# Two cross-attentions on one core: the small algebra in four parts, and a reordered front

## The reference, cut to what matters

```
att = softmax(q k^T / 4) v        # 16 heads; q from x, k and v from ctx
y   = x + att[0]                  # one 256 x 256 block for all 32 batches
F   = layernorm(y) * w2 + b2      # queries
X   = layernorm(ctx) * w1 + b1    # keys and values
A   = softmax(F X^T / 16) X       # 32 batches
h   = gelu(A @ fc1^T + fc1_b)     # 4 features wide
c   = h @ fc2^T + fc2_b
n   = layernorm(c) * w3 + b3
s   = softmax(n n^T / 16) n
out = F + gamma2 * (c + gamma1 * s)
```

## Time and profile before

| | us |
| --- | --- |
| median of 3 runs | 240.56 |
| lowest and highest | 238.62, 248.52 |
| the profiled execution: time | 240.99 |
| its span, first to last instruction | 239.2 |
| PE, DVE, ACT, POOL busy | 213.3, 188.0, 151.0, 139.9 |
| mean granted TensorE clock, share of full | 0.957 |

### The profile page before, as it was taken

One profiled execution on the slowest core, in us unless ns is written; L12 is line 12 of the kernel. 1 busy time (PEld: TensorE's weight loads), 2 busy tenths in 40 slices (PEclk: granted clock), 3 DMA queues, 4 the chain that ended last, 5 costly groups with the idle time before them and its releaser, 6 DMA issues.

```text
span 239.2 us, 4947 instructions
## 1 busy us (share of the span) xinstructions
PE 213.3 (89%) x1736; PEld 153.9 (64%) x1736; DVE 188.0 (79%) x363; ACT 151.0 (63%) x292; POOL 139.9 (58%) x212
## 2 busy tenths in 40 slices
PE   6999989697999999999999989999997499899750
PEld 6766656574977969779698786877684254455320
DVE  6888876999999988968799998971354655988773
ACT  2067774406678858678586995876587346777520
POOL 6000068576999999979959993900028888222330
PEclk9999999979999999999999999999999956999995
DMA  6990000055550454415455000000000004264458
GB/s 191 380 348 7 1 1 3 3 182 169 167 179 29 162 171 176 152 51 160 171 171 174 6 3 1 3 0 1 3 0 3 1 13 165 106 243 182 176 205 325
DMA packets 14712, 26.81 MB, mean 112 GB/s; under 512 B 1760, under 2 KB 1760, under 8 KB 14688
## 3 DMA queue, kind: packets, MB, share of 16 engines
q1 hardware_dynamic: 14688, 26.50, 32.3%
HBM read 18.11 MB, written 8.39 MB: 111 GB/s over the span
## 4 chain that ended last, share of the span: by engine, by line
PE 58%; DVE 24%; POOL 7%; issue 5%; ACT 5%; DVEq 0%; ACTq 0%; POOLq 0%
PE psum L1040 15%; PE psum L977 7%; DVE bn L372 6%; DVE xN L392 5%; PE psum L1048 5%; PE psum L932 3%; DVE Fall L586 3%; PE psum L1078 2%; PE psum L1155 2%; PE psum L990 2%; PE psum L1060 2%; PE psum L1188 2%; PE psum L947 2%; PE psum L1005 2%; PE psum L1018 2%
## 5 line engine op out<-in xcount | busy, mean ns | idle before, releaser
L1040 PE MATMUL psum<-XT,Fall 128*128 128x256 f32 x256 | 62.5, 389 | 1.7 <-ACT Fall L822 1.7
L1040 PEld LDWEIGHTS psum<-XT,Fall 128*128 128x128 f32 x256 | 47.3, 195 | 7.5 <-ACT Fall L822 2.2
L665 POOL TENSOR_SCALAR cN<-cN,nmean,rstd 128x256 f32<-128x256 f32 x64 | 38.2, 608 | 2.4 <-POOL rstd L652 2.3
L645 POOL TENSOR_TENSOR xN<-xN,tgt 128x512 f32<-128x512 f32 x28 | 35.7, 1277 | 1.6 <-DVE xN L392 1.6
L392 DVE TENSOR_SCALAR xN<-xN,bn,rstd 128x256 f32<-128x256 f32 x64 | 34.0, 575 | 0.7 <-POOL rstd L652 0.7
L845 ACT ACTIVATE PT<-psum 128x512 f32<-128x512 f32 x32 | 19.2, 599 | 24.3 <-PE psum L1048 24.2
L652 POOL TENSOR_TENSOR rstd<-vps,minus_half 128x8 f32<-128x8 f32 (+1 forms) x16 | 25.0, 1564 | 15.7 <-DVE vps L383 15.6
L852 ACT ACTIVATE E<-psum,nmax 128x256 f32<-128x256 f32 x64 | 26.8, 474 | 11.0 <-DVE nmax L531 10.9
L531 DVE TENSOR_REDUCE nmax<-psum 128x2 f32<-128x512 f32 x32 | 21.9, 685 | 13.9 <-PE psum L1040 13.4
L571 DVE TENSOR_REDUCE nm<-psum 128x4 bf16<-128x1024 f32 x16 | 19.5, 1221 | 12.0 <-PE psum L1123 12.0
L819 ACT ACTIVATE XT<-psum,b1s,w1s 128x512 f32<-128x512 f32 x32 | 23.1, 792 | 3.7 <-PE psum L977 3.7
(11 more groups left out here) (174 smaller groups left out, 361.0 us busy)
## 6 DMA issues: line engine op xcount, KB each, us to landing
cN<-ctx SPq DMA_DIRECT2D x32, 256.0 KB, 2.9
xN<-x SPq DMA_DIRECT2D x32, 256.0 KB, 4.0
out<-Fall SPq DMA_DIRECT2D x32, 256.0 KB, 2.3
x0T<-x0t SPq DMA_DIRECT2D x1, 256.0 KB, 2.7
wqT<-wqt SPq DMA_DIRECT2D x1, 256.0 KB, 3.2
c0T<-c0t SPq DMA_DIRECT2D x1, 256.0 KB, 3.8
wkT<-wkt SPq DMA_DIRECT2D x1, 256.0 KB, 5.6
wvT<-wvt SPq DMA_DIRECT2D x1, 256.0 KB, 5.8
```

The lines of the kernel that those rows point to most:

```text
L645: pool.tensor_tensor(xN[:, b % SLOTS, :], xN[:, b % SLOTS, :], tgt2[:, :, :].rearrange("p t d -> p (t d)"), ALU.add).then_inc(y_ok, 1)
L665: pool.tensor_scalar(own, own, nmean[:, p % 4, NT * m + t:NT * m + t + 1], root_of(p, 0, m, t), ALU.add, ALU.mult)\
L1040: last = pe.matmul(bank[SBANK1[b % 3]][:, t * N:(t + 1) * N], Fall[:, b, c, t * P:(t + 1) * P], XT[:, p % 4, c, m * N:(m + 1) * N], start= ...
```

## The change

**The algebra.** It is done in four parts of 16 tiles. `hidden_input(0)`, `hidden(0)` take three parts (48 tiles) at once, in slots 27 and 29; part 3 has its own in the second attention (`hidden_input(1)` on DVE behind `maxima(1)`, `hidden(1)` on ACT behind `maxima_turned(2)`). The product with K is taken from h by POOL (`keyed`, 5 columns wide) and multiplied by the inverse root afterwards, in DVE's `left(k)`, which also adds K's last column. Parts 0 and 1 have their squares, variances and roots on DVE, parts 2 and 3 on POOL. `turn(p)` waits for left and right parts at p = 0, 4, 8 and 12; `turn(0)` moves from slot 30 to 31, `turn(1)` and `scores(0)` from 31 to behind the last batch.

**The front.** EARLY is 4: four pairs have the context treated in stage one, where each pair has its own variances and its own root. K is projected and masked in halves, value projections move, x0T and c0T are issued by ACT, and SP issues all context batches ahead of x. The output operand is computed by POOL and not by DVE. `project(0)` and `project_back(0)` come ahead of the slots, with the matmuls for Q and K between them, and slots 0 to 3 of DVE have an order of their own. POOL's addition 5 waits for four normalized batches.

```diff
-LATE = {20: (0,), 22: (1,), 23: (2,), 24: (3,), 25: (4,), 26: (5,), 27: (6,), 28: (7,), 29: (8,)}
+PART = TILES // 4
+SHARES = (slice(0, 3 * PART), slice(3 * PART, TILES))
+KEYED = (4, 8, 16, 24)
+EARLY = 4
...
-        output_operand(0)
-        dve.wait_ge(k_mm, 1)
-        for e, m in enumerate(("even", "odd")):
-            dve.tensor_scalar(kTm[:, e, :, :], tiles(bank[1]), c_(m), None, ALU.mult).then_inc(kT_ok, 1)
-        dve.wait_ge(qk_mm, 1)
-        output_operand(1)
+        def masked(o):
+            dve.wait_ge(k_mm, o + 1)
+            for e, m in enumerate(("even", "odd")):
+                dve.tensor_scalar(kTm[:, e, o, :], bank[(1, 5)[o]][:, 0:N], c_(m), None, ALU.mult).then_inc(kT_ok, 1)
+        masked(0)
...
+                if p == 0:
+                    masked(1)
+                statistics(p, 0)
+                if p % 2 == 1:
+                    first_variances(p // 2)
...
+        def left(k):
+            G = members(k)
+            dve.wait_ge(summed_ok, KEYED[k])
+            if k >= 2:
+                dve.wait_ge(rooted_ok, 7 * (k - 1))
+            link(dve.tensor_tensor(uK[:, G, :], uK[:, G, :], spread(r3[:, G], U), ALU.mult))
+            link(dve.tensor_tensor(uK[:, G, :], uK[:, G, :],
+                                   K[:, U * (U - 1):U * U].unsqueeze(1).to_broadcast([P, PART, U]), ALU.add))
             left_cuts(uK[:, G, :], cut[:, G, 0:U], sU[:, 0, G, :], U)
...
+        dve.wait_ge(qk_mm, 1)
+        link(dve.tensor_copy(Q[:, :], bank[7][:, 0:(H + 1) ** 2]))
+        link(dve.tensor_copy(K[:, :], bank[7][:, 64:64 + U * U]), "QK")
         normal(0)
...
-            if k + 3 < PAIRS:
+            if b >= 4 and k + 3 < PAIRS:
                 statistics(b + 6, 0)
                 statistics(b + 6, 1)
...
+            if b == 0:
+                statistics(5, 1)
+                variances(2)
+            elif b == 1:
+                statistics(6, 1)
+                normal(4)
+                normal(5)
+                statistics(7, 1)
+                variances(3)
+            elif b == 2:
+                statistics(8, 0)
+                statistics(8, 1)
+                normal(6)
+                normal(7)
+            elif b == 3:
+                statistics(9, 0)
+                statistics(9, 1)
+                variances(4)
+            elif k + 2 < PAIRS:
                 normal(b + 4)
-            for part in LATE.get(b, ()):
-                algebra(0, part)
+            if b == 27:
+                hidden_input(0)
+            if b == 29:
+                squares(0)
+                variance(0)
+            if b == 30:
+                scaled(0)
+            if b == 31:
+                left(0)
...
+        squares(1)
         maxima(0)
         saved(QUADS - 1)
+        variance(1)
+        scaled(1)
         for p in range(2 * QUADS + 5):
             if p + 1 < PAIRS:
                 maxima(p + 1)
...
+            if p == 0:
+                left(1)
+                hidden_input(1)
+            if p == 5:
+                left(2)
+            if p == 9:
+                left(3)
             if p >= 5:
                 finish(p - 5)
-            if p == 0:
-                algebra(1, 0)
-            if p == 4:
-                second_keyed(0)
-                second_left(0)
-            if p == 7:
-                second_left(1)
...
+            if b == 5:
+                pool.wait_ge(zy_ok, 8)
...
+        keyed(0)
+        keyed(1)
         right(0)
-        weights5()
-        scaled(0)
+        squares(2)
         right(1)
+        keyed(2)
+        scaled(2)
         output_cuts(0)
-        scaled(1)
+        right(2)
+        pool.wait_ge(gelu_ok, 2)
+        squares(3)
         output_cuts(1)
-        keyed(1)
-        right(2)
-        for q in range(2, QUADS):
+        scaled(3)
+        output_cuts(2)
+        right(3)
+        keyed(3)
+        for q in range(3, QUADS):
             output_cuts(q)
...
+            if b == 29:
+                hidden(0)
             if b >= 1:
                 weights_copied(b - 1)
             exponentials(b)
-            if b == 21:
-                hidden(0)
...
-            if p == 1:
+            if p == 2:
                 hidden(1)
...
-        keep_busy(11, 7)
+        project(0)
+        operand_products()
+        keep_busy(3, 0)
+        project_back(0)
+        keep_busy(4, 0)
         turned(0, 1)
```

More of the change, by code:

```diff
@@ L270, in _ @@
         sp.dma_start(par[:, :], params).then_inc(par_in, 16)
[L271 to L277, removed]
+        sp.dma_start(wqT[:, :, :], wqt).then_inc(q_in, 16)
+        sp.dma_start(wkT[:, :, :], wkt).then_inc(k_in, 16)
+        sp.dma_start(wvT[:, :, :], wvt).then_inc(v_in, 16)
+        for src, dst, arrived in ((c_d, cN, c_in), (x_d, xN, x_in)):
+            for b in range(SLOTS):
+                sp.dma_start(dst[:, b, :], src[b, :, :]).then_inc(arrived[b], 16)
+        for p in range(SLOTS // 2, PAIRS):
+            sp.wait_ge(t_mm, turns_to(p - SLOTS // 2, 1))
             for src, dst, arrived in ((c_d, cN, c_in), (x_d, xN, x_in)):
@@ new lines, in variance @@
+        def variance(k):
+            G = members(k)
+            w5, v, y = W5[:, G, :], var[:, G], r3[:, G]
+            link(dve.tensor_tensor(w5, w5, ha[:, G, :], ALU.mult))
+            link(dve.tensor_reduce(v, w5, AX.X, ALU.add))
+            link(dve.tensor_scalar(v, v, EPS, None, ALU.add))
+            link(dve.tensor_scalar(y.bitcast(I32), v.bitcast(I32), 1, None, ALU.logical_shift_right))
+            link(dve.tensor_scalar(y.bitcast(I32), y.bitcast(I32), -1.0, RSQRT_SEED, ALU.mult, ALU.add))
@@ new lines, in scaled @@
+        def scaled(k):
+            G = members(k)
+            for _ in range(NEWTON):
+                newton(var[:, G], r3[:, G], t3[:, G])
+            link(dve.tensor_tensor(u[:, G, 0:H + 1], ha[:, G, :], spread(r3[:, G], H + 1), ALU.mult), ("u", k))
+        def left(k):
+            G = members(k)
+            dve.wait_ge(summed_ok, KEYED[k])
[4 more added lines that the diff above has]
+                                   K[:, U * (U - 1):U * U].unsqueeze(1).to_broadcast([P, PART, U]), ALU.add))
+            left_cuts(uK[:, G, :], cut[:, G, 0:U], sU[:, 0, G, :], U)
+            ALG["left", k] = count[0]
@@ L523, in _ @@
         normal(3)
-        statistics(5, 1)
-        variances(2)
         def maximum(b):
@@ L782, in _ @@
     def _(act):
+        act.dma_start(x0T[:, :, :], x0t).then_inc(q_in, 16)
+        act.dma_start(c0T[:, :, :], c0t).then_inc(k_in, 16)
         act.wait_ge(q_mm, 1)
@@ L941, in _ @@
         last.then_inc(mean_mm, 1)
-        for arrived, n, w, src, b, done in ((q_in, 32, wqT, x0T, 0, q_mm), (k_in, 32, wkT, c0T, 1, k_mm)):
-            pe.wait_ge(arrived, n)
-            for o in range(2):
-                for c in range(DC):
-                    last = pe.matmul(bank[b][:, o * N:(o + 1) * N], w[:, c, o * P:(o + 1) * P], src[:, c, :],
-                                     start=c == 0, stop=c == DC - 1)
-            last.then_inc(done, 1)
+        pe.wait_ge(q_in, 32)
+        for o in range(2):
+            for c in range(DC):
+                last = pe.matmul(bank[0][:, o * N:(o + 1) * N], wqT[:, c, o * P:(o + 1) * P], x0T[:, c, :],
+                                 start=c == 0, stop=c == DC - 1)
+        last.then_inc(q_mm, 1)
+        pe.wait_ge(k_in, 32)
+        for o in range(2):
+            for c in range(DC):
+                last = pe.matmul(bank[(1, 5)[o]][:, 0:N], wkT[:, c, o * P:(o + 1) * P], c0T[:, c, :],
+                                 start=c == 0, stop=c == DC - 1)
+            last.then_inc(k_mm, 1)
         def operand_products():
@@ L1212, in _ @@
                 weights_turned(b - 1)
+            if b == B:
+                scores(0)
+                turn(1)
             if b == 29:
                 pe.wait_ge(evac_ok, 62)
-                pe.wait_ge(alg, ALG["stR"])
+                pe.wait_ge(operand_ok, ALG["stR"])
                 for c in range(DC):
```

275 lines of the change are left out of this document (113 added, 162 removed).

## The result

The changed kernel takes **259.61 us** (median of 4 runs, 259.08 to 261.53), the kernel before 239.75 beside it. The ratio is **1.083**, interval 1.078 to 1.087: 8% slower, and 10 us above the upper end of the range. Executions of one kernel fall into a faster and a slower state; every ratio here is taken over the faster ones, against the kernel before run beside it, so it can differ a little from the quotient of two medians. The profiled execution took 259.79 with a span of 258.0.

A forecast was written before the change was run, and what follows sets the result against it. PE bounds 60 to 116 us; later DVE and POOL chains set the pace. Stage one -1.15, to slot 6 -1.65, slots 20 to 28 -1.2, second attention +8.0: +4.0 on 240.99 gives 245.0 us, range 238 to 249.5.

The forecast's parts named there:

- the last of POOL's paragraph: Second attention: part 3's keys at 215.6, after maxima 10; DVE waits about 2 us; maxima 11 at 218.6, 8.0 late.
- rival E: Second attention: clock stays up, POOL's chain still binds, maxima 3 at 187.3; 241 to 243 us; chance 0.15.
- Rival C: Second attention: slow clock comes twice, PE standing again before left 3 or during hidden 1; 4 more, 249; chance 0.15.
- the sum: DVE's chain, slot 31 to maxima 2: left 0 and left 1 counted at 1.8 us each.
- its +8.0: Second attention: lateness of maxima 11, with DVE waiting about 2 us for POOL's keys of part 3; end follows at old pace.
- The prediction's own sign that its sum was too low: Second attention: if PE waits for left 1 or left 2 instead of left 3, the sum is too low.
- the 4.0 counted: Front's gain, taken off the forecast's dates: 1.15 stage one, 1.65 to slot 6, 1.2 slots 20 to 28.
- The wait of about 1 us ahead of slot 6: Slot 6: PE waits about 1 us for POOL's two normalizations, because the root stands behind two additions.
- The end of stage one: Stage one: first scores 2.05 early, part given back to added DVE steps, leaving 1.15; ends 2.05 and 0.
- The walk: The forecast's dates followed through the kernel, from the front to the end of the second attention, to a span of 243.3.
- POOL's five terms: POOL's work behind output cuts 0: cuts three times, right twice, squares, scaled, keyed: 5.5 + 4.8 + 2.4 + 5.1 + 2.7 = 20.4.
- rival B: Second attention: keyed 3 ends before maxima 10, no slow clock, DVE's order binds; 238.7, front's far ends 236.0; chance 0.20.

The follow-up runs named there:

- the filled kernel: Changed kernel with idle PE matmuls at four waits (ahead of left 0, at maxima 1, during hidden 1, ahead of left 2): 250.37 us, ratio 1.043.
- `after_fill4`: The filled kernel under its file name: changed kernel with idle matmuls at four PE waits; 250.37 us, ratio 1.043.
- `fill4_quiet`: Changed kernel with the four fillers, and POOL's squares(2) held back until DVE has finished left 0: median 251.89 us (247.67 to 257.55).
- the front alone: Kernel before with only the front of the change, the algebra left as before: 239.39 us against 240.51, ratio 0.995.
- the two kernels where keyed 3 ended before maxima 10: Changed kernel with four fillers and POOL's right 2, squares 3 moved ahead of output cuts 0: 247.47 us; the same plus DVE's variance 1, scaled 1 moved earlier: 247.72 us.
- The five kernels with the four fillers: Changed kernel with four fillers: alone 250.37 us, squares(2) held back 251.89, DVE's queue reordered 247.81, POOL's queue reordered 247.47, both reordered 247.72.
- `before_fill`: Kernel before with 11 idle matmul calls ahead of the first output cuts, where PE stood 3.24 us: 239.42 us against 240.51, ratio 0.997.

## Why the prediction was wrong

**The step that failed** is the last of POOL's paragraph: "Maxima 10 could be through by 213.7: at full clock the pairs come at 2.85 us", with "the end follows at the old pace". From maxima 2 to 10 the forecast had 27.8 and the trace 33.32; from 11 to 15 11.4 and 16.07. Those two are 10.2 of the 14.7 by which the span was missed, and the filled kernel, with the clock up, has 26.01 and 12.46. The forecast had the waits that bring PE to a stand (DVE's 3.4 ahead of maxima 1, hidden 1, left 3), but it let the clock fall once, behind the first of them, and charged about one microsecond for that: maxima 3 at 188.2, against 187.3 in rival E. From maxima 4 on it reckoned with full clock. The clock fell four times: around 170, around 185, from 193 to 200, and for the 30.6 us from 206.9 on.

**Rate and length.** Rival C had the mechanism and 4 us for another stretch of ten. The rate was not too small: from maxima 7 to 15 the changed kernel takes 34.77 us and the filled one 26.85, so 7.9 for 30.6 us, or 0.26 per us, less than C's 0.4. The length was. I had no row for how long such a stretch lasts when PE's work fills it. Why this one lasted three times as long as before's is open: PE was full in both (29.70 of 30.60 and 9.90 of 10.00), so how full it looks doesn't tell them apart, and its length isn't fixed by the wait it begins behind: the wait of 2.3 us for left 3 was followed by half clock from about 215.6 to 219 in `after_fill4`, and from 214.3 to the end, 41 us, in the profile of `fill4_quiet`.

**Small steps beside GpSimd.** Left 0 took 3.1 us and left 1 3.4, where the sum had 1.8 each. The rows of L380, 170 to 817 ns, had shown such a spread; I used it for stage one and left it out at the seam. The interval to maxima 0 was 2.5 longer than forecast: left 0 was 1.3 over, and the half clock behind it is the larger part of the rest (1.5 came back when it was filled); the one to maxima 2 was 1.7 longer, 1.6 of it left 1.

**Left 3 and POOL's last keys.** The interval from maxima 10 to 11 was forecast at 6.1 and measured 5.86, but that is luck. The forecast let DVE stand about 2 us for keyed 3, and this wait is the core of its +8.0. In the changed kernel keyed 3 ended at 219.03, late against 211.6 but before maxima 10 were through at 220.17; DVE stood 1.01 for PE's product at half clock instead:

```profile
218.58 0.45 POOL L742 TENSOR_TENSOR uK<-kv 128x96 f32<-128x96 f32 x1
...
221.18 0.21 DVE L576 RECIPROCAL rB<-psum 128x8 f32<-128x8 f32 x1 [1.01 <-PE psum L1204]
```

Only with the clock up does DVE wait for keyed 3, 0.91 us, until 212.2. The prediction's own sign that its sum was too low, PE waiting for left 2 instead of left 3, was there: 1.41 for left 2 and 0.52 for left 3.

```profile
205.03 0.38 PE L1148 MATMUL psum<-identb,sU 128*128 128x128 bf16 x4 [1.41 <-issue]
...
223.73 0.59 PE L1148 MATMUL psum<-identb,sU 128*128 128x128 bf16 x4 [0.52 <-issue]
```

**The front** gave 1.0 at slot 31 less than the 4.0 counted. The wait of about 1 us ahead of slot 6 came as forecast (1.18), the four slots without algebra took 14.85 as forecast, and the table loads cost 1.28 each. Stage one and the slots behind it were 0.9 short, and the front alone lost another half microsecond up to slot 31. Inside the 0.9 two errors offset each other. The end of stage one came 2.04 early (the copy at 35.07 against 37.11 before; 1.59 with the front alone), where 1.15 was forecast, and from there to score 6 nothing more was won, where 1.65 was forecast. DVE stood 1.49 for the product that gives Q and K, so its first normalization was only 0.84 early, and the normalizations of batches 4 to 7 took 3.17 and 2.59 for two batches beside POOL:

```profile
43.14 0.18 DVE L491 COPY Q<-psum 128x25 f32<-128x25 f32 x1 [1.49 <-PE psum L991]
...
52.87 3.17 DVE L377 TENSOR_SCALAR xN<-xN,bn,rstd 128x256 f32<-128x256 f32 x4
```

**Right** were the order of events and the side: 15 steps of DVE in 3.3 us ahead of maxima 1, PE at a stand for 2.90 there, hidden 1 ahead of maxima 4, POOL idle for 9.54 before right 1. The walk ends at 243.3 and the filled kernel at 246.3, but that nearness is partly luck: the forecast was 1.8 over from maxima 2 to 10 and short nearly everywhere else. Two sums were off without weight: POOL's five terms give 20.5 and not 20.4, and rival B with the front's far ends gives about 235.4 and not 236.0. Rival B's condition was made true in the two kernels where keyed 3 ended before maxima 10: they took 247.5 and 247.7, not 238.7, since left 0, left 1 and left 3 stay on DVE's path. Rival E (clock up, POOL's chain binding) had 241 to 243 for what measured 250.4.

## What to carry to other kernels

Where an edit adds waits of the matmul engine to a part that already falls to the lower clock, count the stretches it opens and let their length run from one stretch's end to the next wait: with several waits in 40 us, filling one moves the fall to the next, and only filling all of them shows what the clock costs. Work cut into smaller parts pays each part's chain of small dependent steps in full if it sits on the path; look for the wait at the head of an in-order queue first (two lines moved gave 2 us here). Casts and two-input steps of 0.2 to 0.4 us on VectorE are to be priced with a product of GpSimd beside them when one is running.

## What was not expected of the hardware

TensorE stayed at half clock for 30.6 us while it was busy 97% of the time (the 16 products of one `attend` took 1.89 us, 1.05 at full clock). A VectorE step of 0.26 us took 0.94 beside a GpSimd product of 1.01. The five kernels with the four fillers gave executions from 244.2 to 257.6 us, one of them with 41 us at half clock at its end. That stretch begins behind the wait of 2.32 us for left 3; in `after_fill4` the clock fell behind the same wait, 2.31 us there, and was full again from 220 on. How long the clock is down differs from one execution of the same program to the next: the four of `fill4_quiet` had mean granted clocks from 0.91 to 0.97, and one execution of `before_fill` took 274.97 us at 0.74, where the others took 238.9 to 242.5 at 0.96 to 0.98.
